# Order of TensorE's work in one step of an expert stage: both products first, then the next expert number, then three transposes

## The chip, the cores and the metric

The kernel runs on one core of one Trainium2 chip. The metric is the device time of one execution in microseconds; of several executions the median counts.

## The reference

One transformer layer in float32 on 8 sequences of 256 tokens with 256 features: attention (16 heads in 4 groups, a causal bias), a residual sum and a layernorm, then a mixture of experts, a residual sum and a layernorm. The change lies in the experts. Their part of the reference, cut:

```python
scores = sigmoid(xf @ gate_w.T)                 # 2048 tokens, 32 experts
w, idx = ...                                    # best 6 of the 4 best groups of 8
c = zeros((T, E)).at[arange(T)[:, None], idx].add(w / sum(w) * 2.5)
g = einsum('td,eid->tei', xf, w11)              # 256 -> 128 per expert
u = einsum('td,eid->tei', xf, w33)
y = einsum('tei,te,edi->td', silu(g) * u, c, w22)   # 128 -> 256
out = layernorm(x + y + shared(xf))
```

## The kernel before

The kernel is written by hand as five instruction streams (SyncE, TensorE, ScalarE, VectorE, GpSimd) that meet at semaphores. The first part computes attention for the eight sequences, the router, and scatters each token's row six times into a table in memory (`routed`), where each expert has a region. Then the rows are cut into SLOTS = 128 slots of 128 rows; all rows of a slot belong to one expert. The last part gathers the six results of every token and normalizes.

The stage of the slots is what the change touches. Each slot s goes through these operations, each named by the line that its instructions carry in the profile:

- SyncE loads the slot's rows into `xg` (L443), as soon as the slot 8 before has given its buffer back.
- TensorE turns the rows, two transposes (L682, `turn_rows`), and ScalarE copies them into `xgT` (L876).
- TensorE multiplies them with the expert's first weights, gate and up together, 256 columns (L690, `gate_up`). In float32 the profile shows four matmuls for it.
- ScalarE makes silu of the gate half, `eg` (L886); VectorE makes `pick_of` (L1243), then the product `ea` (L1247), a reduction (L1250) and `out_row` (L1260).
- TensorE turns `ea` (L698, `turn_act`), VectorE copies it into `eaT` (L1264).
- TensorE multiplies `eaT` with the expert's second weights (L706, `down`), ScalarE scales the result into `ey` (L892), GpSimd scatters it to `expert_out` (L1337).

The engines run these in a software pipeline. In step k TensorE does `gate_up` for slot k, `turn_rows` for slot k+2, `down` for slot k-2 and `turn_act` for slot k-1, in that order. VectorE does in step k: `pick_of`, `ea` and the reduction for slot k, then `out_row` and `eaT` for slot k-1. The data that one product needs is thus worked on by the other engines while TensorE does other slots' work.

Which weights a matmul reads is known only at run time. The expert numbers of four slots (PACKED = 4) are packed in one word of `packed_tab`. `experts_of` reads such a word into a register of TensorE (L712), `expert_in` shifts and masks one number out of it, and the address of the weights is worked out from it by register instructions. The profile lists these under TensorE's weight-load queue as PEldq. The wait in front of `gate_up` (`xg_copied`) and in front of `down` (`ea_copied`) stands before the first register instruction of its address. A word is read at k = 0 and k = 4, at the head of the step; at k = 0 the word before is read once more, right before `down`, since slots k-2 of steps 0 and 1 belong to it.

`slot_loop` writes the steps out in turns of UNROLL = 8 steps. For TensorE three turns come first, straight (slots 0 to 23), then a Fori loop of six passes with two turns each (slots 24 to 119), then the last slots one by one (120 to 127, and steps 128 and 129 which only drain). A `Turn` holds the number of the turn, as a constant or as a register.

Of the kernel before, what the change touches and what calls it, by code (L numbers as in the profile page):

```python
# [44 lines left out]
SLOTS = TOKENS * TOPK // P + EXPERTS  # L45
# [13 lines left out]
UNROLL = 8  # L59
PACKED = 4  # L60
# [20 lines left out]
class Turn:  # L81
# [3 lines left out]
    def __init__(self, eng, turn, slot=None):  # L85
        self.eng, self.turn, self.slot = eng, turn, slot
        self.first = isinstance(turn, int) and turn == 0
        self.counts = {}

    def count(self, ahead, by):  # L90
# [20 lines left out]
def build(nc, xT, x, wq, wk, wv, wo, bias, consts, gate_w, expert_weights, sw1, sw3, sw2, out):  # L111
    ctx, early = ExitStack(), ExitStack()
    with ctx:
# [197 lines left out]
        def slot_loop(eng, step, apart=1, then=None):  # L311

            for j in range(apart):
                turn = Turn(eng, j)
                for k in range(UNROLL):
                    step(k, turn)
            if then is not None:  # L320
                then()
            with eng.Fori(0, (SLOTS // UNROLL - 1 - apart) // 2) as i:
                for j in (apart, apart + 1):
                    turn = Turn(eng, 2 * i + j)
                    for k in range(UNROLL):
                        step(k, turn)
            for s in range(SLOTS - UNROLL, SLOTS + 2):
                step(s % UNROLL, Turn(eng, s // UNROLL, s))

        def load_weights(eng, i):  # L330

# [132 lines left out]
        def _(pe):  # L464
# [211 lines left out]
            def turn_rows(k, turn, ahead):  # L676


                at = (k + ahead) % UNROLL
                turn.wait(pe, rows_loaded, k, ahead, 16)  # L680
                for c in range(KC):
                    last = pe.transpose((KV_BANK, Q_BANK)[at % 2][:, P * c:P * c + P],  # L682
                                        xg[at][:, P * c:P * c + P], ident)
                last.then_inc(xg_turned[at], 1)

            def gate_up(k, turn, e):

                turn.wait(pe, xg_copied, k, 0)
                for c in range(KC):
                    last = pe.matmul(S_BANK[k % 2][:, 0:2 * INTER], xgT[k % 4][:, c, :],  # L690
                                     w13_sb[c][:, bass.ds(e, 1), :].rearrange("p a n -> p (a n)"),
                                     start=(c == 0), stop=(c == KC - 1))
                last.then_inc(gu_ready[k], 1)

            def turn_act(k, turn):
                at = (k - 1) % UNROLL
                turn.wait(pe, e_act, k, -1)
                pe.transpose(T_BANK[at % 2][:, 0:P], ea[at % 2][:], ident).then_inc(ea_turned[at], 1)  # L698

            def down(k, turn, e):  # L700

                at = (k - 2) % UNROLL
                turn.wait(pe, ea_copied, k, -2)
                if not turn.exists(k, 0):
                    turn.wait(pe, ey_ready, k, -4)
                pe.matmul(DOWN[at % 2][:, 0:DIM], eaT[at % 2][:],  # L706
                          w2_sb[:, bass.ds(e, 1), :].rearrange("p a n -> p (a n)"),
                          start=True, stop=True).then_inc(e_down[at], 1)

            def experts_of(word):  # L710

                return pe.value_load(packed_tab[0:1, bass.ds(word, 1)], min_val=0, max_val=EXPERTS ** PACKED - 1)  # L712

            def expert_in(word, k):

                return pe.snap((word >> (5 * (k % PACKED))) & (EXPERTS - 1), min_val=0, max_val=EXPERTS - 1)

            words = {}

            def step(k, turn):  # L720
                first_word = turn.turn * (UNROLL // PACKED)
                if k % PACKED == 0 and turn.exists(k, 0):
                    words[k // PACKED] = experts_of(first_word + k // PACKED)
                if k == 0 and isinstance(turn.turn, int) and turn.turn < W_GROUPS - 1:
                    pe.wait_ge(late_loaded[turn.turn], 16 * W_PARTS)
                if turn.exists(k, 0):
                    gate_up(k, turn, expert_in(words[k // PACKED], k))
                if turn.exists(k, 2):
                    turn_rows(k, turn, 2)
                if turn.exists(k, -2):  # L730
                    if k == 0:
                        words[-1] = experts_of(first_word - 1)
                    down(k, turn, expert_in(words[(k - 2) // PACKED], k - 2))
                if turn.exists(k, -1):
                    turn_act(k, turn)

            for k in range(2):
                turn_rows(k, Turn(pe, 0), 0)
            slot_loop(pe, step, W_GROUPS - 1, lambda: pe.wait_ge(late_loaded[W_GROUPS - 1], 16 * W_PARTS))

            f_banks = [S_BANK[0], T_BANK[0], S_BANK[1], T_BANK[1]]
# [10 lines left out]
        def _(act):  # L752
# [144 lines left out]
            for k in range(2):  # L897
                copy_rows(k, Turn(act, 0), 0)
            slot_loop(act, step)

            f_banks = [S_BANK[0], T_BANK[0], S_BANK[1], T_BANK[1]]
# [26 lines left out]
        def _(dve):  # L928
# [336 lines left out]

            dve.wait_ge(fin_step, FIN_STEPS + 3)
            slot_loop(dve, step)

            f_banks = [S_BANK[0], T_BANK[0], S_BANK[1], T_BANK[1]]
# [134 lines left out]
```

## Time and profile before

| | us |
|---|---|
| median of 3 runs | 661.97 |
| lowest, highest | 658.66, 663.09 |
| profiled execution, its time | 661.51 |
| profiled execution, its span | 659.3 |

The span runs from the first to the last instruction of the core; the run's time holds 2.2 us more around it. The granted TensorE clock over the span is 0.899 of full speed on average, 1.00 in the stage of the slots. The slots take from 367 us to about 607 us of the span. In the views PE is the matmul, PEld its weight load, DVE VectorE, ACT ScalarE and POOL GpSimd. Consecutive instructions of one line are merged in the timeline (x4), with the time from the start of the first to the end of the last; matmuls overlap, so a merged row is longer than the distance to the next.

### The profile page before, as it was taken

How to read it: one execution, taken by the hardware profiler on the slowest of the kernel's cores; microseconds unless marked ns; L12 is line 12 of the kernel's file. 1: busy time of each engine (PE TensorE's matmuls, PEld its weight loads, DVE VectorE, ACT ScalarE, POOL GpSimd, SP SyncE). 2: the span in 40 equal slices, each digit the busy share in tenths (PEclk: the TensorE clock that was granted, in tenths of full speed). 3: DMA queues.
4: the chain of work that ended last, by engine and by line, in shares of the span. 5: the costliest groups of instructions: out<-in, count | busy, mean ns of one | idle time of the engine just before them, and what ended most of it. 6: DMA issues, size and time to landing. Idle time of an engine off the chain costs nothing.

```text
span 659.3 us, 11939 instructions
## 1 busy us (share of the span) xinstructions
PE 508.1 (77%) x2806; PEld 377.9 (57%) x2807; DVE 354.4 (54%) x1744; ACT 331.6 (50%) x1093; POOL 221.9 (34%) x244
## 2 busy tenths in 40 slices
PE   5287787586776867565598998999999999987573
PEld 3165566363544645352354777777777777765453
DVE  3144868291847657365173454555555554544396
ACT  1177988282846748341210455555555555545033
POOL 0000002406060423337324254555555555545000
PEclk9679999788897768598699999999999999999698
DMA  4877598664472812129593344444444444420893
GB/s 128 213 187 215 128 274 217 206 150 155 107 187 83 204 43 92 60 74 395 212 386 104 92 146 125 137 130 138 138 139 134 138 143 145 136 71 19 346 416 130
DMA packets 67991, 107.87 MB, mean 164 GB/s; under 512 B 9189, under 2 KB 55018, under 8 KB 66416
## 3 DMA queue, kind: packets, MB, share of 16 engines
q1 hardware_dynamic: 54016, 75.15, 39.7%
q0 software_dynamic: 10752, 26.13, 11.4%
q10 hardware_dynamic: 3184, 6.13, 2.5%
q8 instruction: 18, 0.29, 0.2%
q14 instruction: 21, 0.17, 0.1%
HBM read 64.03 MB, written 43.33 MB: 163 GB/s over the span
## 4 chain that ended last, share of the span: by engine, by line
PE 44%; DVE 20%; another core or an unknown queue 11%; ACT 8%; DMA 7%; issue 7%; SPq 2%; POOL 1%; DVEq 0%; ACTq 0%; POOLq 0%
PE bank L690 17%; PE bank L706 9%; DVE s_neg L967 4%; ACT probs L789 4%; PE bank L682 4%; PE bank L631 3%; DMA k_scratch<-k_lo 2%; DMA k_pack<-k_scratch 2%; PE bank L640 2%; PE bank L698 2%; PE bank L534 2%; ACT pT L800 2%; DMA xt<-xT 1%; PE bank L471 1%
## 5 line engine op out<-in xcount | busy, mean ns | idle before, releaser
L1327 POOL DMA_INDIRECT routed<-rows,position x96 | 93.4, 973 | 258.1 <-DVE position L1118 230.5
L1337 POOL DMA_INDIRECT expert_out<-ey_all,out_row x128 | 125.9, 983 | 129.5 <-ACT ey_all L892 67.5
L789 ACT ACTIVATE probs<-s_neg,m_neg 128x128 f32<-128x128 f32 (+1 forms) x256 | 114.0, 452 | 84.5 <-DVE m_neg L967 77.0
L690 PE MATMUL bank<-expert_w,xgT 128*128 x512 | 135.6, 388 | 10.8 <-issue 10.0
L967 DVE CUSTOM_DVE_ANT_0 s_neg<-bank,bias_sb 128x128 f32<-128x128 f32 (+1 forms) x256 | 78.0, 352 | 95.7 <-remote 60.9
L690 PEld LDWEIGHTS bank<-expert_w,xgT 128*128 128x128 f32 x512 | 87.7, 191 | 35.1 <-issue 21.3
L892 ACT ACTIVATE ey_all<-bank,pick 128x256 f32<-128x256 f32 x128 | 60.7, 474 | 61.6 <-PE bank L706 40.1
L1243 DVE SCALAR_TENSOR_TENSOR pick_of<-xg,slot_e 128x12 f32<-128x12 f32 x128 | 29.8, 233 | 106.9 <-ACT eg L886 91.8
L706 PE MATMUL bank<-expert_w,eaT 128*128 x256 | 80.9, 398 | 5.1 <-DVE eaT L1264 4.4
L503 PE MATMUL bank<-k_pack,q_pack 128*128 128x256 f32 (+1 forms) x128 | 60.9, 485 | 13.8 <-DMA k_pack<-k_scratch 11.2
L517 PE MATMUL bank<-cst,probs 128*128 128x128 f32 x256 | 46.9, 310 | 22.2 <-ACT probs L789 16.0
L886 ACT ACTIVATE eg<-bank 128x128 f32<-128x128 f32 x128 | 35.5, 278 | 48.7 <-PE bank L690 37.9
L534 PE MATMUL bank<-pT,v_sb 128*32 128x128 f32 (+1 forms) x512 | 40.5, 366 | 22.2 <-issue 21.8
L800 ACT ACTIVATE pT<-bank 128x512 f32<-128x512 f32 x96 | 56.2, 587 | 1.1 <-remote 1.1
L876 ACT ACTIVATE xgT<-bank 128x256 f32<-128x256 f32 x128 | 48.1, 376 | 8.5 <-PE bank L682 8.5
L517 PEld LDWEIGHTS bank<-cst,probs 128*128 128x128 f32 x256 | 32.9, 156 | 33.8 <-ACT probs L789 25.8
L789 ACT ACTIVATION_READ_ACCUMULATOR probs<-s_neg,m_neg 128x1 f32 x256 | 50.2, 196 | 0.0
L682 PE MATMUL bank<-cst,xg 128*128 128x128 f32 x256 | 49.0, 274 | 0.6 <-issue 0.6
L706 PEld LDWEIGHTS bank<-expert_w,eaT 128*128 128x128 f32 x256 | 38.6, 190 | 12.0 <-issue 10.4
L682 PEld LDWEIGHTS bank<-cst,xg 128*128 128x128 f32 x256 | 36.1, 142 | 13.8 <-issue 1.1
L534 PEld LDWEIGHTS bank<-pT,v_sb 128*32 128x32 f32 x512 | 18.6, 119 | 42.8 <-issue 38.5
L1264 DVE COPY eaT<-bank 128x128 f32<-128x128 f32 x128 | 36.4, 284 | 5.9 <-remote 3.8
(155 smaller groups left out, 718.5 us busy)
## 6 DMA issues: line engine op xcount, KB each, us to landing
xg<-routed SPq DMA_DIRECT2D x128, 137.5 KB
expert_w<-expert_out SPq DMA_DIRECT2D x16, 768.0 KB
expert_w<-expert_weights SPq DMA_DIRECT2D x9, 1024.0 KB
q_pack<-q_scratch SPq DMA_DIRECT2D x32, 256.0 KB
routed<-empty SPq DMA_DIRECT2D x8, 550.0 KB, 12.2
k_pack<-k_scratch SPq DMA_DIRECT2D x16, 256.0 KB
expert_w<-expert_weights ACTq DMA_DIRECT2D x3, 1024.0 KB
xt<-xT SPq DMA_DIRECT2D x9, 256.0 KB, 6.9
```

The lines of the kernel that those rows point to most:

```text
L503: pe.matmul(SCORES[u][:, 0:2 * n], q_pack[par][:, 2 * g + pair, P * qb:P * qb + P], k_pack[par][:, g, :, 0:n], start=True, stop=True).then ...
L517: last = pe.transpose(pb[:, at:at + P], probs[g % 2][qb][:, r, 0:P], ident)
L534: last = pe.matmul(O_BANK[at:at + 32, P * kb:SEQ], v_sb[par][:, kb, g, col:col + 32], pT[g][:, r, :], start=(kb == 0 and odd == 0), stop=( ...
L682: last = pe.transpose((KV_BANK, Q_BANK)[at % 2][:, P * c:P * c + P], xg[at][:, P * c:P * c + P], ident)
L690: last = pe.matmul(S_BANK[k % 2][:, 0:2 * INTER], xgT[k % 4][:, c, :], w13_sb[c][:, bass.ds(e, 1), :].rearrange("p a n -> p (a n)"), start ...
L706: pe.matmul(DOWN[at % 2][:, 0:DIM], eaT[at % 2][:], w2_sb[:, bass.ds(e, 1), :].rearrange("p a n -> p (a n)"), start=True, stop=True).then_ ...
L789: act.activation(probs[g % 2][qb][:, 2 * pair + r, :], s_neg[u][:, r, 0:n], ACT.Exp, bias=m_neg[:, u, r:r + 1], scale=-1.0, accum_out=row_ ...
L800: act.activation(dst.rearrange("p r t -> p (r t)"), T_BANK[(3 * g + j) % 2][:], ACT.Copy).then_inc(pt_copied, 1)
L892: act.activation(ey[at], DOWN[at % 2][:, 0:DIM], ACT.Copy, scale=pick[:, at, 0:1]).then_inc(ey_ready[at], 1)
L967: dve.tensor_tensor_reduce(out=s_neg[u][:, r, 0:n], in0=SCORES[u][:, n * r:n * r + n], in1=bias_sb[:, REP * g + 2 * pair + r, SEQ - n:SEQ] ...
L1327: pool.indirect_dma_start(routed, bass.IndirectOffsetOnAxis(ap=position[b % ROW_BUFS][:, t, j:j + 1], axis=0), rows[b % ROW_BUFS][:, t, :] ...
L1337: pool.indirect_dma_start(expert_out, bass.IndirectOffsetOnAxis(ap=out_row[:, k:k + 1], axis=0), ey[k], None, bounds_check=TOKENS * TOPK - ...
```

## The change

Only TensorE's stream changes. In a step both products come first (`gate_up` for slot k, `down` for slot k-2), then the number of the next slot's expert is worked out (and its word read, if the next slot is the first of four), then `turn_act` for slot k-1, then `turn_rows` for slot k+2. Numbers are handed on from step to step: `held["next"]` to the next step's `gate_up`, `held["last"]` and `held["before_last"]` to `down`. This goes on across turns that are written out straight behind each other; the first turn of such a run has `opens` set, and there the number of slot 0 and the word before are read as they were. So the word before is read once for each straight run instead of once for each turn.

```diff
@@ class Turn
         self.first = isinstance(turn, int) and turn == 0
+        self.opens, self.next = False, None
         self.counts = {}
@@ slot_loop
-            for j in range(apart):
-                turn = Turn(eng, j)
+            def straight(turns):
+                turns[0].opens = True
+                for turn, following in zip(turns, turns[1:]):
+                    turn.next = following
+                return turns
+
+            for turn in straight([Turn(eng, j) for j in range(apart)]):
                 for k in range(UNROLL):
                     step(k, turn)
             if then is not None:
                 then()
             with eng.Fori(0, (SLOTS // UNROLL - 1 - apart) // 2) as i:
-                for j in (apart, apart + 1):
-                    turn = Turn(eng, 2 * i + j)
+                for turn in straight([Turn(eng, 2 * i + j) for j in (apart, apart + 1)]):
                     for k in range(UNROLL):
                         step(k, turn)
-            for s in range(SLOTS - UNROLL, SLOTS + 2):
-                step(s % UNROLL, Turn(eng, s // UNROLL, s))
+            for turn in straight([Turn(eng, s // UNROLL, s) for s in range(SLOTS - UNROLL, SLOTS + 2)]):
+                step(turn.slot % UNROLL, turn)
@@ TensorE's step
-            words = {}
+            held = {}
+
+            def expert_of(turn, k):
+
+                if k % PACKED == 0:
+                    held["word"] = experts_of(turn.turn * (UNROLL // PACKED) + k // PACKED)
+                return expert_in(held["word"], k)
 
             def step(k, turn):
-                first_word = turn.turn * (UNROLL // PACKED)
-                if k % PACKED == 0 and turn.exists(k, 0):
-                    words[k // PACKED] = experts_of(first_word + k // PACKED)
+                if k == 0 and turn.opens:
+                    held.clear()
                 if k == 0 and isinstance(turn.turn, int) and turn.turn < W_GROUPS - 1:
                     pe.wait_ge(late_loaded[turn.turn], 16 * W_PARTS)
+                now = None
                 if turn.exists(k, 0):
-                    gate_up(k, turn, expert_in(words[k // PACKED], k))
+                    now = held.pop("next") if "next" in held else expert_of(turn, k)
+                    gate_up(k, turn, now)
+                if turn.exists(k, -2):
+                    before_last = held.get("before_last")
+                    if before_last is None:
+                        if k == 0:
+                            held["back"] = experts_of(turn.turn * (UNROLL // PACKED) - 1)
+                        before_last = expert_in(held["back"], k - 2)
+                    down(k, turn, before_last)
+                held["before_last"], held["last"] = held.get("last"), now
+                following = turn if k < UNROLL - 1 and turn.slot is None else turn.next
+                if following is not None and turn.exists(k, 1):
+                    held["next"] = expert_of(following, (k + 1) % UNROLL)
+                if turn.exists(k, -1):
+                    turn_act(k, turn)
                 if turn.exists(k, 2):
                     turn_rows(k, turn, 2)
-                if turn.exists(k, -2):
-                    if k == 0:
-                        words[-1] = experts_of(first_word - 1)
-                    down(k, turn, expert_in(words[(k - 2) // PACKED], k - 2))
-                if turn.exists(k, -1):
-                    turn_act(k, turn)
```

## Rows read from the trace of the kernel before

**Rows 1.** The page: span, and busy time of PE (share, instructions)

```profile
span 659.3 us, 11939 instructions
PE 508.1 (77%) x2806; PEld 377.9 (57%) x2807; DVE 354.4 (54%) x1744; ACT 331.6 (50%) x1093; POOL 221.9 (34%) x244
```

**Rows 2.** Busy time by stretch: from:to, length, each engine, clock, DMA share, GB/s

```profile
380.00:580.00 200.00, 188.48 (x971) 149.28 (x972) 103.31 (x538) 110.58 (x324) 105.71 (x108) 1.00 0.46 137
```

**Rows 3.** Timeline of PE: start, us, line, operation, [idle before it <- releaser]

```profile
440.22 1.13 PE L690 MATMUL bank<-expert_w,xgT 128*128 x4 [0.69 <-issue]
...
441.71 0.69 PE L706 MATMUL bank<-expert_w,eaT 128*128 x2 [0.15 <-issue]
...
442.35 1.03 PE L690 MATMUL bank<-expert_w,xgT 128*128 x4
443.22 0.38 PE L682 MATMUL bank<-cst,xg 128*128 128x128 f32 x2
443.44 0.60 PE L706 MATMUL bank<-expert_w,eaT 128*128 x2
443.87 0.27 PE L698 MATMUL bank<-cst,ea 128*128 128x128 f32 x1
443.98 1.03 PE L690 MATMUL bank<-expert_w,xgT 128*128 x4
...
445.06 0.60 PE L706 MATMUL bank<-expert_w,eaT 128*128 x2
...
446.69 0.60 PE L706 MATMUL bank<-expert_w,eaT 128*128 x2
...
447.70 1.12 PE L690 MATMUL bank<-expert_w,xgT 128*128 x4 [0.30 <-issue]
...
453.85 0.69 PE L706 MATMUL bank<-expert_w,eaT 128*128 x2
...
454.97 1.13 PE L690 MATMUL bank<-expert_w,xgT 128*128 x4 [0.32 <-issue]
...
456.19 0.69 PE L706 MATMUL bank<-expert_w,eaT 128*128 x2
...
458.06 0.69 PE L706 MATMUL bank<-expert_w,eaT 128*128 x2
...
468.43 0.66 PE L706 MATMUL bank<-expert_w,eaT 128*128 x2
...
469.86 1.13 PE L690 MATMUL bank<-expert_w,xgT 128*128 x4 [0.67 <-issue]
```

**Rows 4.** Timeline of all engines, from 443.4 to 445.0 us

```profile
443.42 0.28 ACT L886 ACTIVATE eg<-bank 128x128 f32<-128x128 f32 x1 [0.23 <-PE bank L690]
...
443.84 0.23 DVE L1243 SCALAR_TENSOR_TENSOR pick_of<-xg,slot_e 128x12 f32<-128x12 f32 x1 [0.92 <-ACT eg L886]
...
443.99 0.28 DVE L1247 TENSOR_TENSOR ea<-bank,eg 128x128 f32<-128x128 f32 x1
...
444.41 0.22 DVE L1260 SCALAR_TENSOR_TENSOR out_row<-pick,again,xg 128x1 int32<-128x1 f32 x1
...
444.54 0.28 DVE L1264 COPY eaT<-bank 128x128 f32<-128x128 f32 x1
...
444.96 0.30 PEld L706 LDWEIGHTS bank<-expert_w,eaT 128*128 128x128 f32 x2
```

**Rows 5.** L706 from 444.8 to 445.2 us: ns min/median/max, first and last start

```profile
L706 PEldq FUSED_REGOPS  x1: 46/46/46, 444.9 to 444.9; - x1
```

**Rows 6.** L712, the read: from 446.6 to 447.5 us, and over the whole span

```profile
L712 PEldq TENSOR_LOAD <-packed_tab x1: 432/432/432, 446.7 to 446.7; - x1
...
L712 PEldq TENSOR_LOAD <-packed_tab x48: 297/312/543, 366.1 to 603.9; - x48
```

**Rows 7.** Timeline of all engines, from 457 to 458.2 us: eaT in step 0

```profile
457.37 0.29 DVE L1264 COPY eaT<-bank 128x128 f32<-128x128 f32 x1
```

## Prediction

> **What bounds the kernel now.** I read the page first: the profiled execution spans 659.3 us and TensorE (PE) is its busiest engine [rows 1]. The change touches only PE's program for the 128 slots, so the second view is the busy time by stretch: from 380 to 580 us PE is busy 188.5 of 200 us at a granted clock of 1.00, DVE 103, ACT 111, POOL 106 [rows 2]. So PE is the bound of this stage, and the question is what fills the 11.5 us in which it is idle, and what else the matmuls wait for.
>
> The third view is PE's own timeline, for one step [rows 3]. The expert products (L690) start at 442.35; the two transposes (L682) at 443.22, which is 0.87 later; the second product (L706) at 443.44, 0.22 later; the transpose of L698 0.43 after that (443.87) and the next L690 0.11 later, at 443.98. The period is 0.87 + 0.22 + 0.43 + 0.11 = 1.63 us, and in it PE never stops: that is the floor of a step. (A first matmul after a stall is drawn 0.10 longer, x4 1.13 instead of 1.03 and x2 0.69 instead of 0.60. I take its true start as 0.10 after the one printed, and 0.66 as 0.06.)
>
> The fourth view, all engines over the same step, shows what the second product needs [rows 4]. L690 of slot k starts at 442.35 and is drawn to 443.38. ACT's silu starts at 443.42, DVE's pick_of at 443.84, ea at 443.99, out_row at 444.41, and only then eaT of the slot before, 444.54 to 444.82; DVE does these in order, so eaT(k-1) hangs on L690(k). The weights of L706 load at 444.96 and its matmul starts at 445.06. The register instruction ahead of it (FUSED_REGOPS of L706) stands at 444.9 [rows 5], so PE's sequencer sits at this wait. **From the start of L690(k) to the earliest start of the product of k-1 is X = 445.06 - 442.35 = 2.71 us.** The order of before asks for that product at 1.63 + 0.87 + 0.22 = 2.72 us. It fits with 0.01 us to spare.
>
> The sequencer matters for the reads of the packed expert numbers (L712). A read is a TENSOR_LOAD, 0.43 us in the one I follow and 0.30 to 0.54 among all 48 [rows 6], with register work around it. At 446.69 L706 starts and the next L690 truly at 447.80: 1.11 us where 0.54 is normal, so 0.57 is lost [rows 3]. Two Fori turns (16 slots, 440.32 to 469.96 true, 29.64 us) split so: 16 x 1.63 = 26.04, rest 3.60. First turn: the extra read of the word before, 440.32 to 441.81, 1.49 for a normal 1.09: 0.40; read for k=4 0.57; 0.18 of late eaT at k=7; read for the next turn, 453.95 to 455.07, 1.12 for 0.54: 0.58. Second turn: extra read 455.07 to 456.29: 0.13; late L706 at 458.16 true, period 1.87: 0.24; loop end with its branch, 468.49 to 469.96, 1.47 for 0.54: 0.93; what is left, 0.57, is the read for k=4 (0.51) and 0.06 of late eaT.
>
> **The change part by part.**
>
> *The second product moves ahead of the row transposes.* It is now asked for at one period + 0.87 after L690(k), 2.50 us in an unstalled step, and eaT still comes through the chain of [rows 4] at X = 2.71. None of that chain moves: silu waits for L690 only, and turn_act(k-1) is issued 0.43 after the second product starts, well before DVE gets to eaT. After the second product come 0.11 + 0.22 + 0 us of transposes, then the next L690. So each period is T = 0.76 + max(0.87, X - previous T). From 1.63 the next is 0.76 + 1.08 = 1.84; from 1.84 the next is 1.63 again. **Two steps cost 3.47 instead of 3.26: 0.22 us every second step**, unless a read has just made the step before long. Near k=0 and k=7 X is larger. For k=0: L690 true 455.07, eaT ends at 457.66 [rows 7], plus the 0.24 from eaT's end to the matmul of [rows 4]: 2.83. For k=6 in the first turn: 2.71 + the 0.18 above, 2.89; in the second 2.77.
>
> *The read stands before the three transposes.* Its cover was the second product and one transpose, 0.54 us. It is now the second product alone, 0.43, because the sequencer still reaches the read only when the wait for eaT lets go. Behind the read the mask alone stands before the first transpose, where mask and address stood before L690. One register instruction lies in the 0.14 from eaT's end (444.82) to L706's weights (444.96) [rows 4], so it is worth 0 to 0.14; I take 0.10. A read then costs 0.57 + 0.11 - 0.10 = 0.58. Queued behind it are turn_act and turn_rows; the next L690's address work hides under their 0.33. The bounds: 0.30 and 0.54 for the load instead of 0.43 [rows 6] make it 0.45 to 0.69. At the loop end no read is made ahead, and the three transposes cover it too: 0.93 - 0.22 = 0.71.
>
> A rule of the Trainium skill bears on this. "Perfetto Trace Analysis", section Sequencer Loop, says that engine instructions are pushed into a queue and wait there, while control instructions execute in the sequencer itself. The trace agrees: L706's register instruction stands at 444.9, after eaT's end at 444.82 [rows 4, 5], and the read comes after it. By the rule a wait at a transpose does not hold a read up and the wait before an address does, which leaves the sum as it is worked out here; were waits before addresses queued too, the sum would be that of rival B.
>
> *Fewer reads.* Of the 48 reads 32 are of the slots' own words and 16 of the word before (turns 1 to 15 and step 128). These stay only where a straight run opens, once per pass of the loop and once for the last slots: 7, so 39 in all. It now has L690 alone as cover, so 0.40 + 0.22 = 0.62, say 0.60. In the second turn 0.13 and 0.24 go.
>
> *The number of the next slot is worked out before the transposes in every step.* Two register instructions, 0.2 us by the 0.10 above, under the 0.43 of the second product: nothing. Without that cover it would be 0.2 us a step.
>
> The sum over two turns. First turn: opening read 0.60; k=2 late 0.22; read 0.58; k=5 late 0.22; k=7 late 2.89 - 1.63 - 0.87 = 0.39; read 0.58: 2.59. Second turn: k=1 late 2.83 - 2.50 = 0.33; k=3 late 0.22 and read 0.58, less 0.06 because the mean read there was cheaper; k=5 late 0.22; k=7 late 0.27; loop end 0.71: 2.27. Together 4.86 for 3.60: **+1.26 us per 16 slots**, +7.6 for the six passes. The first 24 slots are three turns of the second kind without a branch: late steps 1.04, less 0.43 that goes, so about +0.6 each for two and +0.2 for the first: +1.4. The last 8 slots open a run: +0.2 for the read and three late steps of 0.22: +0.9. Sum +9.9 us. Behind the slots the final stage waits for the last sends, so nothing gives this back. Profiled 661.5 (span 659.3) becomes 671.4; the median of the runs shown, 661.97, lies 0.5 above the profiled one: **672 us**.
>
> **Rivals.**
>
> A, *same*: X is shorter in the new order by 0.21 or more (say because DVE or ACT is less in the way). Then no step is late and only reads change: 0.60 + 0.58 + 0.58, and 0.52 + 0.71, is 2.99 for 3.60, -0.6 x 8 = -5: 657 us. For it: 0.2 us is little. Against: the chain is made of durations and of waits on itself, with no idle share that the transposes caused.
>
> B, *faster*: eaT comes so early that the sequencer is no longer held at the second product. Then the read (about 1.0 us from the weights of L706 to the next instruction) runs under both products, 1.30 us, and the reads cost nothing; the opening one and the loop end stay, 0.60 + 0.71 = 1.31 for 3.60: -2.3 x 8 = -18: 644 us. It decides from the point where eaT is ready some 0.6 us before it is asked for (1.0 - 0.43). Against: [rows 4] has it 0.01 us ahead with the order that leaves it 0.22 more.
>
> C, *much slower*: no step recovers, each is late by at least 0.22 but the 5 of 16 that follow a read. In the forecast the late steps make 0.22 + 0.22 + 0.39 + 0.33 + 0.22 + 0.22 + 0.27 = 1.87; here 11 x 0.22 and 0.33 for the longer waits, 2.75: +0.9 x 8 = +7, and with reads at 0.69 +3: 682 us. Against: the late step itself gives the next one 0.22 more time.
>
> D, *the reads get the cheap load* (0.30 instead of 0.43), some 26 behind the second product: 26 x 0.13 = 3.4 off, 668.6, the edge of what counts as the same.
>
> **Chances.** My forecast with D 0.76, A 0.12, B 0.05, C 0.07. The likeliest one's own range is 667 to 677: reads at 0.45 or 0.69 (-3.4, +2.9) and 2 us for the first and last turns. The range is 661 to 679, which leaves out B, C and most of A. About 1% (6.6 us) is what a measurement of this kernel can tell from no change; below 655.4 it is faster, above 668.6 slower. Slower: C and seven eighths of the forecast, 0.74. Same: A for the most part and D's edge, 0.19. Faster: B and a bit of A, 0.07.
>
> **What the changed profile would show.** Starts of L690 inside a turn alternate 1.63 and 1.84 (1.63, 1.96, 1.63, 2.4, 1.63, 1.84, 1.63, 2.5 in the second turn). L706's weight load follows eaT's end by 0.14 in the long steps, and PE is idle there for about 0.2 us where it wasn't. Sixteen slots take 30.9 us for 29.6. L712 has 39 TENSOR_LOADs for 48. A gap of about 0.6 stands between L706 and L698 at k=3 and k=7. I am wrong in size if L690 to eaT is not 2.47 us any more, and wrong in sign if L706 follows L690 in every step without a gap.

## The result: 0.8% slower, half of what was forecast

The changed kernel is slower than the kernel before by a ratio of 1.0078 (95% interval 1.0054 to 1.0103). Side by side, 15 runs each, the medians are 663.99 and 659.07 us (three of the 15 runs before are those that the prediction started from, with a median of 661.97). The forecast was +10 us, the result is +5. The direction, the place and the mechanism of the loss were as forecast; the price of the reads and of the last slots was not.

Line numbers moved: the expert products are L695 (was L690) and L711 (L706), the transposes L687 (L682) and L703 (L698), the read L717 (L712), eaT's copy L1283 (L1264), silu L905.

The page of the changed kernel, span and busy time:

```profile
span 665.4 us, 11869 instructions
PE 520.2 (78%) x2806; PEld 377.9 (57%) x2807; DVE 355.7 (53%) x1744; ACT 334.0 (50%) x1093; POOL 222.1 (33%) x244
```

The busy time from 380 to 580 us (columns as in [rows 2]):

```profile
380.00:580.00 200.00, 190.95 (x947) 141.47 (x947) 102.19 (x527) 109.94 (x316) 103.34 (x106) 1.00 0.46 134
```

Against [rows 1] and [rows 2] this reads oddly: PE is busier (190.95 us for 188.48) and does less (947 matmuls for 971 in the same 200 us). PE's share is no measure here: matmuls overlap in the drawing, and the ones behind a short gap are drawn 0.10 us longer, which fills it. The weight loads tell it better, 141.5 us busy for 149.3.

The stage of the slots, first and last matmul of L695:

```profile
L695 PE MATMUL bank<-expert_w,xgT x512: 379/379/478, 368.4 to 609.0; 128*128 x171
```

By true starts (a first matmul behind a stall counted 0.10 us later than drawn) L690 ran from 367.4 to 602.8 for slot 127, L695 runs from 368.5 to 608.3: 239.8 us for 235.4, +4.4 us. The two profiled executions are 6.1 us apart, since the one of the changed kernel is among its slower ones (667.62 us); 1.1 us of that lies ahead of the slots and 0.6 behind them. So the slots hold most of the difference.

PE's timeline over one pass of the loop; to be held against [rows 3]:

```profile
442.91 1.12 PE L695 MATMUL bank<-expert_w,xgT 128*128 x4 [0.75 <-issue]
...
444.97 1.03 PE L695 MATMUL bank<-expert_w,xgT 128*128 x4
...
446.81 1.03 PE L695 MATMUL bank<-expert_w,xgT 128*128 x4
...
448.44 1.03 PE L695 MATMUL bank<-expert_w,xgT 128*128 x4
449.43 0.69 PE L711 MATMUL bank<-expert_w,eaT 128*128 x2
450.33 0.32 PE L703 MATMUL bank<-cst,ea 128*128 128x128 f32 x1 [0.20 <-issue]
...
450.71 1.03 PE L695 MATMUL bank<-expert_w,xgT 128*128 x4
...
452.33 1.03 PE L695 MATMUL bank<-expert_w,xgT 128*128 x4
...
454.18 1.03 PE L695 MATMUL bank<-expert_w,xgT 128*128 x4
...
455.81 1.03 PE L695 MATMUL bank<-expert_w,xgT 128*128 x4
...
456.98 0.69 PE L711 MATMUL bank<-expert_w,eaT 128*128 x2
457.77 0.33 PE L703 MATMUL bank<-cst,ea 128*128 128x128 f32 x1
...
458.15 1.03 PE L695 MATMUL bank<-expert_w,xgT 128*128 x4
...
473.22 1.13 PE L695 MATMUL bank<-expert_w,xgT 128*128 x4 [0.55 <-issue]
```

The true starts of the first turn are 1.96, 1.84, 1.63, 2.27, 1.62, 1.85, 1.63 and 2.34 us apart; 16 slots take 473.32 - 443.01 = 30.3 us (29.6 before). The second turn reads 1.62, 1.96, 1.62, 2.14 to 2.27, 1.62, 1.85, 1.62, 2.7 in the four passes in the middle of the loop. The short and the late periods without a read (1.62, 1.85, 1.96) are those that were forecast, to 0.01 us. The periods with a read (2.4 and 2.5 were forecast for the second turn) and the place of the late steps in the first turn are not.

All engines, one late step (to be held against [rows 4]):

```profile
449.00 0.28 DVE L1283 COPY eaT<-bank 128x128 f32<-128x128 f32 x1
...
449.42 0.30 PEld L711 LDWEIGHTS bank<-expert_w,eaT 128*128 128x128 f32 x2 [0.36 <-issue]
```

and the register instruction ahead of L711, and the read behind it:

```profile
L711 PEldq FUSED_REGOPS  x1: 46/46/46, 449.3 to 449.3; - x1
```

```profile
L717 PEldq TENSOR_LOAD <-packed_tab x1: 429/429/429, 449.6 to 449.6; - x1
```

eaT ends at 449.28, the register instruction follows, the weights load at 449.42, and the true start is 449.53, 2.72 us after the L695 at 446.81. X, the time from the start of the first product of slot k to the earliest start of the second product of slot k-1, was 2.71 before: the chain did not change, the order asks for its end 0.22 us too soon.

### The profile page after: what moved, and what is told of

It is laid out like the page before. It is cut to its first block, busy times and chain, and to the rows that moved or that the text cites. A ratio compares the mean times of both kernels' runs of the same rounds, so it can differ in the third digit from the quotient of the medians.

```text
span 665.4 us, 11869 instructions
## 1 busy us (share of the span) xinstructions
PE 520.2 (78%) x2806; PEld 377.9 (57%) x2807; DVE 355.7 (53%) x1744; ACT 334.0 (50%) x1093; POOL 222.1 (33%) x244
## 4 chain that ended last, share of the span: by engine, by line
PE 46%; DVE 17%; ACT 10%; another core or an unknown queue 9%; issue 8%; DMA 8%; SPq 2%; POOL 1%; DVEq 0%; ACTq 0%; POOLq 0%
PE bank L695 14%; PE bank L711 9%; ACT probs L808 5%; PE bank L636 4%; PE bank L687 4%; DVE s_neg L986 3%; PE bank L703 2%; DMA k_scratch<-k_lo 2%; PE bank L539 2%; PE bank L645 2%; DMA k_pack<-k_scratch 2%; ACT pT L819 2%; PE bank L476 2%; DMA xt<-xT 1%
## 5 line engine op out<-in xcount | busy, mean ns | idle before, releaser
L695 PE MATMUL bank<-expert_w,xgT 128*128 x512 | 132.7, 382 | 3.7 <-issue 3.1
L695 PEld LDWEIGHTS bank<-expert_w,xgT 128*128 128x128 f32 x512 | 87.2, 190 | 12.4 <-issue 5.5
L1262 DVE SCALAR_TENSOR_TENSOR pick_of<-xg,slot_e 128x12 f32<-128x12 f32 x128 | 29.6, 232 | 113.5 <-ACT eg L905 93.2
L711 PE MATMUL bank<-expert_w,eaT 128*128 x256 | 83.3, 407 | 6.5 <-issue 2.5
L911 ACT ACTIVATE ey_all<-bank,pick 128x256 f32<-128x256 f32 x128 | 60.6, 473 | 40.6 <-PE bank L711 27.6
L905 ACT ACTIVATE eg<-bank 128x128 f32<-128x128 f32 x128 | 35.5, 277 | 64.9 <-PE bank L695 61.8
L522 PE MATMUL bank<-cst,probs 128*128 128x128 f32 x256 | 49.5, 320 | 23.4 <-ACT probs L808 17.3
L711 PEld LDWEIGHTS bank<-expert_w,eaT 128*128 128x128 f32 x256 | 40.8, 188 | 37.7 <-issue 32.8
L539 PE MATMUL bank<-pT,v_sb 128*32 128x128 f32 (+1 forms) x512 | 36.1, 345 | 19.2 <-issue 18.9
L687 PE MATMUL bank<-cst,xg 128*128 128x128 f32 x256 | 48.7, 273 | 0.6 <-issue 0.6
L703 PE MATMUL bank<-cst,ea 128*128 128x128 f32 x128 | 36.1, 282 | 2.9 <-issue 2.0
L539 PEld LDWEIGHTS bank<-pT,v_sb 128*32 128x32 f32 x512 | 17.2, 113 | 36.8 <-issue 31.8
L766 PE MATMUL bank<-expert_w,cst 128*128 128x256 f32 x96 | 26.8, 437 | 14.3 <-DMA expert_w<-expert_out 14.3
```

Source lines behind the costliest of these rows:

```text
L522: last = pe.transpose(pb[:, at:at + P], probs[g % 2][qb][:, r, 0:P], ident)
L539: last = pe.matmul(O_BANK[at:at + 32, P * kb:SEQ], v_sb[par][:, kb, g, col:col + 32], pT[g][:, r, :], start=(kb == 0 and odd == 0), stop=( ...
L711: pe.matmul(DOWN[at % 2][:, 0:DIM], eaT[at % 2][:], w2_sb[:, bass.ds(e, 1), :].rearrange("p a n -> p (a n)"), start=True, stop=True).then_ ...
L911: act.activation(ey[at], DOWN[at % 2][:, 0:DIM], ACT.Copy, scale=pick[:, at, 0:1]).then_inc(ey_ready[at], 1)
```

## The experiments

Not all kernels ran on the same chip. On the chip of e1b, e2b, e3b and e4b the kernel before takes 603 us; on the others it takes 659 to 663. The slots begin at 310 to 319 us in the profiles from the first chip and at 367 to 372 us in the others, so most of the difference lies ahead of them. Whole times are therefore compared as ratios to the kernel before on the same chip, and the stage of the slots by the time that 16 slots take in the middle of the loop, which is a number of PE's timeline.

| kernel | 16 slots, us | ratio to before (95%) |
|---|---|---|
| before | 29.6 | 1 |
| changed | 30.35 | 1.0078 (1.0054 to 1.0103) |
| e1b_rows_between | 29.5 | 0.9988 (0.9951 to 1.0024) |
| e2b_order_only | 30.25 | 1.0092 (1.0052 to 1.0132) |
| e3b_eaT_early | 27.45 | 0.9733 (0.9664 to 0.9801) |
| e4b_read_early | 27.8 | 0.9759 (0.9691 to 0.9828) |
| e6_no_reads | 28.5 | one run, 655.8 us for 663.4 |
| e7_both | 27.5 | 0.9741 (0.9665 to 0.9817) |
| e8_sp_twice | 29.6 | one run, 662.6 us for 663.4 |
| e9_four_turns | 26.8 | 0.9730 (0.9648 to 0.9811) |
| e11_longer_chain | 30.5 | 1.0094 (1.0066 to 1.0122) |
| e3c_again | 27.45 | 0.9770 (0.9716 to 0.9824) |

**The row transposes back between the products.**

```diff
 # TensorE's step of the changed kernel
                     gate_up(k, turn, now)
+                if turn.exists(k, 2):
+                    turn_rows(k, turn, 2)
                 if turn.exists(k, -2):
 ...
                     turn_act(k, turn)
-                if turn.exists(k, 2):
-                    turn_rows(k, turn, 2)
```

> The changed kernel with turn_rows back between the two products: gate_up, turn_rows, down, next number (and its read), turn_act. Theory (late steps): the loss of the change comes from asking for eaT 0.22 us earlier than it can be there. With the rows back between the products the periods of 1.85 go, the reads keep their cheaper place, and 16 slots take 28.8 us (30.35 in the changed kernel, 29.6 before): 5 to 7 us under the kernel before. Rival (the place of the read behind down is what costs): as slow as the changed kernel, 5 us over the kernel before, 16 slots about 30.3.

The late steps without a read are gone, as the first theory says: the periods at k=1 and k=5 of the opening turn are 1.63 us (1.84 and 1.85 in the changed kernel), and the ones of the second turn 1.74 and 1.63 (1.96 and 1.85). The kernel is level with the one before, so the place of the read alone is not what made the change slow. The number was missed: 29.5 us, not 28.8, and no gain where 5 to 7 us were expected. The reads are dear again. PE's timeline at a read:

```profile
402.38 0.60 PE L711 MATMUL bank<-expert_w,eaT 128*128 x2
403.16 0.33 PE L703 MATMUL bank<-cst,ea 128*128 128x128 f32 x1 [0.18 <-issue]
403.37 0.91 PE L695 MATMUL bank<-expert_w,xgT 128*128 x3
```

L703 follows 0.84 us (true) after L711, as in the changed kernel (0.85). But the next L695 comes at 403.47 (true), 0.26 after L703 where 0.11 is normal. The register instructions of L695 in that stretch:

```profile
L695 PEldq FUSED_REGOPS  x2: 46/46/46, 403.3 to 403.4; - x2
L695 PEldq ALU_OP  x1: 32/32/32, 403.2 to 403.2; - x1
```

The mask and the address of L695 are worked out here, behind L703, one transpose before they are needed. In the changed kernel they stand there too (ALU_OP of L695 at 450.4, behind L703's weights), but two more transposes hide them. So the read costs 1.09 - 0.54 = 0.55 here and 0.42 there.

**Only the order of the products.**

```diff
 # TensorE's step of the kernel before
-                if turn.exists(k, 2):
-                    turn_rows(k, turn, 2)
                 if turn.exists(k, -2):
 ...
                 if turn.exists(k, -1):
                     turn_act(k, turn)
+                if turn.exists(k, 2):
+                    turn_rows(k, turn, 2)
```

> The kernel before with nothing but the order changed: gate_up, down, turn_act, turn_rows; all 48 reads where they were, at the head of steps 0 and 4 and before down at step 0. Theory: late steps as in the changed kernel (about 1.0 us per turn of 8), reads at the heads 0.2 cheaper each because three transposes cover them, the extra reads 0.2 dearer: 16 slots about 30.8 us, 7 to 9 us over the kernel before. Rival (the new place of the reads costs, not the order): within 2 us of the kernel before.

It loses what the whole change loses (0.9%, 16 slots 30.25 us), but less than I had put down: 30.8 us and 7 to 9 us in all were expected, 0.9% of 603 is 5.5. Moving the reads and dropping nine of them therefore brought nothing measurable: a read at the head of a step gets the cover of three transposes, one behind the second product does not.

**eaT copied early.** TensorE's program stays that of the change but for the value that turn_act waits for. VectorE does out_row at the head of the step and copies eaT between pick_of and ea:

```diff
+                # head of VectorE's step: out_row of k-1, once its reduction is in
+                turn.wait(dve, e_act, k, -1, 2)
+                dve.scalar_tensor_tensor(out_row[:, at:at + 1], ...)
                 dve.scalar_tensor_tensor(pick_of[k % 2][:], ...)
+                turn.wait(dve, ea_turned, k, -1)
+                dve.tensor_copy(eaT[at % 2][:], ...).then_inc(ea_copied[at], 1)
                 dve.tensor_tensor(ea[k % 2][:], ...).then_inc(e_act[k], 1)
-                turn.wait(dve, e_act, k, 0)
-                dve.tensor_reduce(pick[:, k, :], ...)
-                ... out_row, then eaT of k-1
+                need(dve, e_act[k], turn.odd())     # 2 * turn + 1
+                dve.tensor_reduce(pick[:, k, :], ...).then_inc(e_act[k], 1)
```

> The changed kernel, TensorE's program as it is; VectorE copies eaT of the slot before between pick_of and ea, and does out_row at the head of its step, so three of its operations leave the chain from L695 to the copy of eaT. Theory: from the start of L695 to the earliest product of the slot before falls from 2.71 to about 2.2 us, below the 2.50 at which the product is asked for. The long periods of 1.85 go, and the sequencer is released some 0.3 us before the product is due, so the reads at steps 3 and 7 cost 0 to 0.15 instead of 0.31 to 0.42. 16 slots 26.9 to 27.4 us, 16 to 20 us under the kernel before. Rival (something else sets the long periods, such as ScalarE's copies or the queue of TensorE): no change against the changed kernel, 5 us over the kernel before. Second rival: GpSimd's sends, 1.63 to 1.7 us apart when they follow each other, become the bound: 16 slots not below 26.9.

The theory holds: 16 slots take 27.45 us, just over the 26.9 to 27.4 that were expected, and the whole is 16 us shorter. PE and DVE in one step:

```profile
393.45 0.23 DVE L1280 SCALAR_TENSOR_TENSOR pick_of<-xg,slot_e 128x12 f32<-128x12 f32 x1 [0.45 <-ACT eg L912]
...
393.59 1.03 PE L702 MATMUL bank<-expert_w,xgT 128*128 x4
393.60 0.28 DVE L1267 COPY eaT<-bank 128x128 f32<-128x128 f32 x1
...
394.24 0.41 PEld L718 LDWEIGHTS bank<-expert_w,eaT 128*128 128x128 f32 x2
...
395.22 1.03 PE L702 MATMUL bank<-expert_w,xgT 128*128 x4
```

eaT ends at 393.88, 0.36 us before the weights load; the period is 1.63. The sequencer is let go early too: the periods with a read (k=3, k=7 of the first turn) are 1.62 to 1.65, one of 1.73 apart. This is rival B of the prediction, reached by moving eaT. What is left over the floor is the start of a pass (2.1) and its end (2.6); all other periods are at TensorE's own floor, so GpSimd's sends are not the bound. e3c_again is the same kernel on one of the other chips.

> The kernel with eaT copied early again, now beside the kernel before on the same chip as the run with the longer chain. Theory: 16 slots 27.5 us again, 15 to 18 us under the kernel before, whatever the chip's own time for the attention part is. Rival (the gain seen was the other chip's): less than half of that.

16 slots 27.45 and -14 us (647.5 for 661.6): the middle of the loop is the same; the whole fell 1 us short of the range. The two ends of the loop are not the same. On the first chip the loop's first step takes 2.12 us and the first two steps behind it 3.5 together; here it is 3.55 and 8.2.

**The read before the wait.**

```diff
 # on top of the rows between the products
+                following = turn if k < UNROLL - 1 and turn.slot is None else turn.next
+                if following is not None and turn.exists(k, 1):
+                    held["next"] = expert_of(following, (k + 1) % UNROLL)
                 if turn.exists(k, -2):
                     ...
                     down(k, turn, before_last)
                 held["before_last"], held["last"] = held.get("last"), now
-                following = ...
```

> gate_up, turn_rows, next number (and its read), down, turn_act: the read stands before the wait for eaT instead of behind it. Theory (the sequencer is held at the wait before down, so a read behind it has only down as cover): the reads at steps 3 and 7 now run under gate_up and cost 0 to 0.1, and no step is late. What is left over 26.04 are the read where a run opens (0.3 to 0.4), the end of the loop (0.9) and 0.3 of late eaT at steps 0, 6, 7: 16 slots 27.6 us, 13 to 16 us under the kernel before. Rival (a read costs its length wherever it stands, because it waits for the queue to drain): the same as with the read behind down, 28.8 us for 16 slots.

27.8 us (27.6 expected) and -2.4%, which is 14.5 us: as expected, and the rival is out. The period with a read at k=3 is 1.63 us; at k=7 of the first turn it is 1.80, and the 0.17 over the floor is late eaT, not the read (L695 to L711 is 1.26 for 1.09). L711 waits no differently than before (start of L695 to L711 1.09), and the same read that cost 0.42 or 0.55 behind that wait costs nothing ahead of it:

```profile
396.65 1.03 PE L695 MATMUL bank<-expert_w,xgT 128*128 x4
397.74 0.60 PE L711 MATMUL bank<-expert_w,eaT 128*128 x2
398.28 1.03 PE L695 MATMUL bank<-expert_w,xgT 128*128 x4
```

**No reads at all.** experts_of returns the number of its word, and the shift in expert_in (not shown) is one bit a slot instead of five. This kernel leaves out the reads and with them the right expert numbers: the matmuls take the weights of wrong experts.

```diff
-                return pe.value_load(packed_tab[0:1, bass.ds(word, 1)], ...)
+                return word
```

> The changed kernel without the reads of packed expert numbers: experts_of gives the number of the word itself, from which each step's number is shifted and masked, so the matmuls take the weights of wrong experts, with all register work but the read and what belongs to it. Left out: the reads alone. Theory: what stays over the floor of 1.63 a step are the late steps. Periods alternate 1.63 and 1.85 through the whole turn, with 1.9 at k=0/1 and 6/7, and 16 slots take 27.9 to 28.2 us (30.35 in the changed kernel): the reads cost 2.2 us of 16 slots, the late steps 2.0. Rival (the long periods are an after-effect of the reads' stalls): without them all periods are 1.63 and 16 slots take 26.1 to 26.5 us.

PE's timeline, three steps:

```profile
455.87 1.03 PE L695 MATMUL bank<-expert_w,xgT 128*128 x4
456.97 0.69 PE L711 MATMUL bank<-expert_w,eaT 128*128 x2
...
457.83 1.03 PE L695 MATMUL bank<-expert_w,xgT 128*128 x4
458.70 0.59 PE L711 MATMUL bank<-expert_w,eaT 128*128 x2
...
459.46 1.03 PE L695 MATMUL bank<-expert_w,xgT 128*128 x4
460.45 0.69 PE L711 MATMUL bank<-expert_w,eaT 128*128 x2
...
461.30 1.03 PE L695 MATMUL bank<-expert_w,xgT 128*128 x4
```

1.96, 1.63, 1.84: the late steps need no read. That rules out the rival, 26.1 to 26.5 us. 16 slots take 28.5 us, 0.3 over the expected range; the start of a pass keeps 0.2 + 0.4. So in the changed kernel 30.35 - 28.5 = 1.85 us of 16 slots are reads and 28.5 - 26.05 = 2.45 are late steps and the loop's own instructions.

**Both cures.** The diff of eaT early on top of the read before the wait.

> The kernel with the read before down (e4b_read_early) and with eaT copied early (as in e3b_eaT_early): gate_up, turn_rows, next number, down, turn_act, the loop of two turns. Theory: both cures act on the same loss. The read costs nothing in either, and late eaT is down to 0.3 us per 16 slots in e4b, so adding the early copy brings at most 0.3 to 0.6 us per 16 slots: 2 to 4 us under e4b_read_early, level with e3b_eaT_early within 2 us. Rival (the two losses were separate and add): 10 us or more under either.

They don't add: 27.5 us, 0.3 under e4b_read_early and level with e3b_eaT_early, as expected. Both take the same thing away, the read behind a wait that ends at the last moment.

**A longer chain in the kernel before.**

```diff
                     dve.scalar_tensor_tensor(out_row[:, at:at + 1], pick[:, at, 1:2], ...)
+                    dve.scalar_tensor_tensor(spare[:, at:at + 1], pick[:, at, 1:2], ...)
                     turn.wait(dve, ea_turned, k, -1)
```

> The kernel before, TensorE's program untouched; VectorE does out_row's operation a second time, into a tile that nobody reads, so the copy of eaT comes about 0.1 to 0.22 us later. VectorE has room for it (1.2 of 1.63 us a step). Theory: in the kernel before the product is asked for only 0.01 us after it can start, so this alone brings the long periods: with 0.22 us more, 1.84 and 1.63 in turn as in the changed kernel (1.73 and 1.63 with 0.1), 16 slots 30.3 to 31.1 us for 29.6, and 5 to 11 us over the kernel before. Rival (the long periods belong to the order of TensorE's instructions, not to when eaT is ready): a VectorE operation that lies in its idle time costs nothing, within 1.5 us of the kernel before.

+0.94%, 6 us, and 16 slots 30.5 us, both inside the expected range. The kernel before, with TensorE's program untouched, gets the late periods of the changed one:

```profile
452.02 1.03 PE L691 MATMUL bank<-expert_w,xgT 128*128 x4
...
452.71 0.28 DVE L1268 COPY eaT<-bank 128x128 f32<-128x128 f32 x1
...
453.13 0.30 PEld L707 LDWEIGHTS bank<-expert_w,eaT 128*128 128x128 f32 x2
...
453.77 1.03 PE L691 MATMUL bank<-expert_w,xgT 128*128 x4
```

The added operation moves eaT 0.13 us, and the period shown is 1.75 (1.63 before). Periods of 1.75 and 1.63 follow each other where no read stands. This is the sharpest test: an operation in VectorE's idle time costs 6 us, because it lies on the one path without slack.

**Longer passes.** TensorE's loop of four turns, three passes, on top of eaT early.

```diff
-            with eng.Fori(0, (SLOTS // UNROLL - 1 - apart) // 2) as i:
-                for turn in straight([Turn(eng, 2 * i + j) for j in (apart, apart + 1)]):
+            with eng.Fori(0, (SLOTS // UNROLL - 1 - apart) // per) as i:
+                for turn in straight([Turn(eng, per * i + apart + j) for j in range(per)]):
```

> The kernel with eaT copied early (e3b_eaT_early) with TensorE's loop of four turns a pass, three passes, instead of two turns, six passes. In e3b an end of the loop costs 0.95 us and the read of the word before in the first step of a pass 0.48; the other reads cost nothing. Theory: each pass saved takes 1.4 us with it, less nothing for the new places, 3 x 1.4 = 4.3 us under e3b_eaT_early. Rival (the longer body costs more at its end or in loading instructions than is saved): equal or slower than e3b_eaT_early.

Inside the loop it does what was expected in one of three passes: 32 slots 53.6 us for 54.9. The last pass takes 54.1, with one period of 2.68 that I can't explain. As a whole it is level (0.9730 for 0.9733 and 0.9770) where 4.3 us less were expected: entry and exit of the loop are dear. At the exit PE's timeline has

```profile
574.17 1.12 PE L702 MATMUL bank<-expert_w,xgT 128*128 x4
576.20 0.69 PE L718 MATMUL bank<-expert_w,eaT 128*128 x2 [0.91 <-issue]
...
579.15 1.12 PE L702 MATMUL bank<-expert_w,xgT 128*128 x4 [1.93 <-ACT xgT L902]
```

4.99 us for a step that takes 1.63. Single profiles differ there by 1 to 2 us between kernels whose TensorE program is the same (the first two steps behind the loop take 6.75 us in the kernel before, 5.1 in e8, 6.6 in e11), so I can't say how much of it the longer body adds.

**The length of a read.** SyncE reads its address twice.

```diff
+                sp.value_load(slot_tab[0:1, bass.ds(s, 1)], ...)
                 at = sp.value_load(slot_tab[0:1, bass.ds(s, 1)], ...)
```

> The kernel before, in which SyncE reads its slot's address twice in a row (the first value is not used). In both traces TensorE's read takes about 0.30 us, but 0.40 to 0.54 where a read of SyncE starts within 0.1 us before to 0.2 us after its start. Theory (two register loads at the same time lengthen each other): with twice as many reads of SyncE more of TensorE's 48 reads are long, 28 or more for 24, and each long one overlaps a SyncE read in its first 0.3 us; none is long without one. Rival (the length follows from what TensorE or ScalarE do at that moment): the same slots' reads are long as before, whether SyncE reads or not. The time changes by less than 3 us either way.

The theory falls in the form that was expected: with twice as many reads of SyncE 19 of TensorE's 48 reads are 0.38 us or longer, not 28 or more (20 in the kernel before). Two of the 19 overlap no read of SyncE, and in e4b 14 of the 17 reads that begin beside one of SyncE's (0.1 us before its start to 0.2 us after) are short. But the two go together all the same. Over the eleven profiles with reads, 112 of the 275 that overlap a read of SyncE are long, and 10 of the 187 that don't.

That a read takes 0.30 or 0.43 us depends on the moment (at k=7 of the first turn it was 0.45 to 0.47 in five of six passes before and is 0.31 now in all six). An overlap with a read of SyncE is not enough to make it long; what is, stays open.

## Why the prediction was right in kind and wrong in size

*What bounds the kernel, and X.* Right. The second product was asked for 0.01 us after it could start, and X stayed at 2.71 to 2.72. e11 shows that this margin was all there was: 0.13 us more in the chain made 0.12 us more in the period. e3b shows that it was the chain through VectorE.

*The recurrence T = 0.76 + max(0.87, X - previous T).* Right: 1.63 and 1.85 in turn, 1.96 at k=1, and 2.02 at k=7 of the first turn once the read's 0.31 is taken off. It gave +0.33, 0.22, 0.22 and 0.27 in the second turn, and the trace has 0.33, 0.22, 0.22 and 0.27. In the first turn one thing was missing. k=1 became late (0.21) and k=3 with it, where k=2 was forecast, so the late steps of that turn are 1.04 for the 0.83 of the sum. Where a turn opens, the number for the second product is masked out of the word before, behind the wait for eaT:

```profile
445.32 0.28 DVE L1283 COPY eaT<-bank 128x128 f32<-128x128 f32 x1
...
445.95 0.30 PEld L711 LDWEIGHTS bank<-expert_w,eaT 128*128 128x128 f32 x2 [0.35 <-issue]
```

```profile
L711 PEldq ALU_OP  x2: 36/36/36, 445.6 to 445.7; - x2
```

With three register instructions (the two shown and FUSED_REGOPS) instead of one, the weights load 0.35 us after eaT's end and not 0.14, and X is 3.05 us there. The opening step at the forecast price, 2.23 us, would have hidden that (2.23 + 0.87 = 3.10); at the 1.97 that it took it could not. The kernel before has the same three instructions at this place, and the row transposes hid them.

*The read at 0.58.* This is the step that failed, together with the opening read below: the mechanism held, but the prediction put too high a price on a read behind the second product. Measured: L711 truly at 449.53, L703 truly at 450.38 (drawn 0.05 long), 0.85 - 0.43 = 0.42 at k=3; at k=7 of the first turn 457.82 - 457.08 = 0.74 - 0.43 = 0.31. Three parts: I let the mask stand in front of the first transpose, while it is issued behind the transposes, at L695 (0.10); I took the delay of a first matmul behind a stall from a product (0.10), and for a transpose it is 0.05, so 0.05 too much; and the load at k=7 takes 0.31 instead of 0.43 to 0.46 (0.13). The bound of 0.45 that I gave was still too high, since it varied the load alone. At k=3 of the second turn the read costs 0.30, forecast at 0.52. e1b, where no further transpose covers mask and address, has 0.55.

*The opening read at 0.60.* Measured 0.34 (period 1.97 for 1.63). The load takes 0.30 us for the 0.42 of before, and it starts 0.25 us after the drawn start of L695, where it was 0.42 after L690 when the row transposes stood between them. *The loop end at 0.71* was 0.81.

In a pass in the middle of the loop the opening read is 0.26 under the sum and the three other reads 0.16, 0.27 and 0.22; the late steps of the first turn are 0.21 over it and the loop end 0.10. That makes 30.3 us where 30.9 was forecast, and 3.6 us over six passes. In the profiled pair all six passes together take 182.5 us for 178.6, +3.9 where +7.6 was forecast.

*The first 24 slots at +1.4.* Measured 43.1 for 41.8: +1.3, right. *The last 8 at +0.9.* Measured, from the first product of slot 120 to that of slot 127, 14.15 for 14.96: -0.8. With the six passes this is the miss of the profiled pair: +1.3, +3.9 and -0.8 are the +4.4 of the slots, for +9.9. The first two steps behind the loop are 3.97 and 2.78 us long in the profile before and 3.42 and 2.44 now. Before:

```profile
587.76 1.13 PE L690 MATMUL bank<-expert_w,xgT 128*128 x4 [0.33 <-issue]
...
590.66 1.16 PE L706 MATMUL bank<-expert_w,eaT 128*128 x2 [1.55 <-DVE eaT L1264]
...
591.83 1.92 PE L690 MATMUL bank<-expert_w,xgT 128*128 x4
...
594.60 1.03 PE L690 MATMUL bank<-expert_w,xgT 128*128 x4
```

```profile
590.80:594.10 3.30, 3.30 (x10) 2.55 (x11) 0.63 (x5) 1.03 (x3) 1.71 (x2) 0.50 0.28 77
```

Now:

```profile
594.07 1.12 PE L695 MATMUL bank<-expert_w,xgT 128*128 x4
...
597.50 1.11 PE L695 MATMUL bank<-expert_w,xgT 128*128 x4
...
600.02 1.03 PE L695 MATMUL bank<-expert_w,xgT 128*128 x4
```

The granted clock of 1.00 that was read for the stage of the slots holds from 380 to 580 us. Right behind the loop, from 590.8 to 594.1 us, the kernel before ran at 0.50 (1.2 GHz), after 1.55 us in which PE stood idle and waited for eaT; an L690 is drawn 1.92 us long there, for 1.03. The changed kernel's profile has 1.00 there (2.4 GHz), although PE idled 1.45 us at the same place. From the true start of the L706 at 590.76 to the L690 at 594.60 it is 3.84 us, and 0.54 + 1.63 = 2.17 at full clock, so the lower clock cost the profile before about 1.7 us. Without it the last slots would have come out at about +0.9, as forecast. One pair of profiles can't settle that, since the waits there vary as well: of the other profiles from these chips e11, e3c and e9 have the stretch at 0.50 behind the loop, e6, e7 and e8 don't, and the two steps take 3.60 and 3.04 us in e11, 3.48 and 1.63 in e8, and 3.3 to 3.5 together on the faster chip. The term should have stood in the range with ±1.5.

*The rivals.* A, B and C were given small chances and did not come. But e3b and e4b show that B's mechanism is real: a read costs nothing once the sequencer is not held at the second product, whether eaT comes earlier or the read stands ahead. D, cheaper reads, is the one that came, and larger than I had it: only some of the reads got the cheap load (29 of 39 took less than 0.38 us, against 28 of 48 before), and mask, transpose and opening read were cheaper on top. The measured +0.8% lies inside 1%, an outcome that was given 0.19.

*The rule on waits.* The reads were priced by a sequencer that is held at the wait before L706's address. e4b bears this out: the same read costs nothing ahead of that wait. The Trainium skill ("Perfetto Trace Analysis", Sequencer Loop) has engine instructions pushed into a queue, where they wait for their semaphores, and control instructions executed by the sequencer itself. e4b agrees with that.

## What to carry to other kernels

Before an instruction is moved ahead in a software pipeline, measure from its producer's start to the earliest moment its data can be there, and hold it against the moment at which each order asks for it; here 0.01 us of slack was left and 0.22 was taken. Here the busy share of the bounding engine even rose, and the loss showed as alternating periods. A register load belongs ahead of the next wait that stands before an address, not behind it, and what is worked out from it should have matmuls still to be drawn between it and its use; both cures here (27.45 and 27.8 us for 29.6) gave 2.3 to 2.7%, where the order of the products alone lost 0.9%.

## What the runs showed of the hardware

A first matmul behind a stall is drawn 0.10 us longer for the products (x4 1.13 for 1.03) and 0.05 longer for a transpose (0.32 for 0.27). The one at 442.91 in the changed kernel is drawn from 0.01 us after its weight load began, which took 0.19, and the next starts 0.32 us later where 0.22 is normal; I read that as a start 0.10 later than drawn. PE's busy time rose by 2.5 us in 200 while it did 24 matmuls less.

At a granted clock of 0.50 (before, 590.8 to 594.1 us) the matmuls of one L690 start 0.43 us apart and are drawn 0.63 long, for 0.22 and 0.38 at 1.00.

A register load on TensorE took 0.30 us in most places and 0.38 to 0.57 in about a quarter of them; nearly all of the long ones overlap a register load of SyncE (112 of 122), but an overlap is not enough to make a load long (163 of 275 stayed short). From the end of the copy that was waited for to the load of the weights it took 0.14 us with one register instruction of TensorE in between and 0.35 with three.

The kernel with eaT early took 587.4 us on one chip and 647.5 on another. In the profiles the slots began at 318.6 and 367.7 us, which is 49 of the 55 us between them; another 6.7 lie in the slots, nearly all of it where the loop begins and right behind it. The loop's first step took 2.0 to 2.1 us on the faster chip (four profiles) and 2.5 to 4.5 on the others (eight), the first two steps behind it 3.3 to 3.5 and 5.1 to 8.2 together. What makes these steps long on the others is open.
